# A one-core graph attention layer: the second head group's end cut into two and two target tiles, the guard moved from a product into the division, and the loop's order dealt anew

## What is computed

```python
h = relu(layernorm(x))
msg = h_neigh[None] + E[edge_types]      # edge_types = adj, so E[1] wherever an edge exists
q = h @ Wq.T + bq;  k = msg @ Wk.T + bk;  v = msg @ Wv.T + bv       # 8 heads x 16
scores = einsum(q, k) / 4, set to -1e9 where adj == 0
attn = softmax(scores) over the neighbours, 0 where adj == 0
out = x + einsum(attn, v).reshape(512, 128) @ Wo.T + bo
```

## Time and profile before

| | |
|---|---|
| three runs | 49.55, 49.84, 50.02 us |
| profiled execution | 49.53 us, span 47.7 us |
| busy | PE 42.2, DVE 39.1, ACT 33.6, POOL 30.0 us |
| first A-score of the stack (L622) | 14.82 us |
| first exponential | 17.59 us |
| last maximum ends | 33.39 us |
| last masked score ends | 40.16 us |
| last turn back ends | 44.70 us |
| last DMA issue | 45.59 us |

### The profile page before, as it was taken

How to read it: one execution, slowest core, us unless ns; L and a number is a source line. 1 busy time by engine, 2 the same in 40 slices (tenths; PEclk the granted TensorE clock), 3 DMA queues, 4 the chain that set the end, 5 groups by cost and what they waited for, 6 DMA issues and landing times.

```text
span 47.7 us, 834 instructions
## 1 busy us (share of the span) xinstructions
PE 42.2 (88%) x253; PEld 17.9 (37%) x256; DVE 39.1 (82%) x110; ACT 33.6 (70%) x60; POOL 30.0 (63%) x53
## 2 busy tenths in 40 slices
PE   0799996889997999999999999999999999999800
PEld 0323234365325244244544352252412233476500
DVE  2694696786898999999999999899788969999400
ACT  0293528689998759999999999599759999200410
POOL 5881005089996999484858579990899999800000
DMA  0499998980099999910000000000000000000032
GB/s 0 81 317 449 399 311 180 406 376 22 0 215 194 192 283 206 204 31 0 0 0 0 7 0 7 0 0 14 0 0 0 0 0 0 0 14 0 0 139 81
DMA packets 2071, 4.93 MB, mean 103 GB/s; under 512 B 258, under 2 KB 786, under 8 KB 1810
## 3 DMA queue, kind: packets, MB, share of 16 engines
q1 hardware_dynamic: 1490, 2.38, 21.2%
q10 hardware_dynamic: 576, 2.49, 13.9%
HBM read 3.02 MB, written 0.26 MB: 69 GB/s over the span
## 4 chain that ended last, share of the span: by engine, by line
PE 65%; DVE 17%; ACT 9%; issue 3%; DVEq 0%
PE ps L655 15%; PE ps L622 10%; PE ps L547 8%; PE ps L672 8%; PE ps L610 7%; DVE masked_scores L476 4%; PE ps L630 4%; PE ps L650 3%; ACT prob L395 3%; DVE turned_U L502 3%; DVE scaled L506 3%; DVE masked_n L491 3%; PE ps L556 2%; DVE ctxT L515 2%; PE ps L578 1%
## 5 line engine op out<-in xcount | busy, mean ns | idle before, releaser
L476 DVE CUSTOM_DVE_ANT_0 masked_scores<-ps,mask_b 128x512 bf16<-128x512 f32 x32 | 19.9, 687 | 0.5 <-PE ps L610 0.3
L260 POOL TENSOR_TENSOR prob<-prob,live 128x512 int32<-128x512 int32 x11 | 13.9, 1279 | 0.0
L395 ACT ACTIVATE prob<-ps 128x512 f32<-128x512 f32 x23 | 12.2, 599 | 1.0 <-PE ps L655 0.8
L655 PE MATMUL ps<-stack 98*128 98x512 bf16 x32 | 11.0, 381 | 0.3 <-issue 0.2
L622 PE MATMUL ps<-stack 96*128 96x512 bf16 x28 | 9.8, 379 | 0.4 <-DMA stack<-split 0.3
L491 DVE TENSOR_TENSOR masked_n<-ps,veto 128x512 f32<-128x512 f32 x9 | 5.7, 684 | 1.0 <-PE ps L655 1.0
L395 ACT ACTIVATE prob<-masked_n 128x512 f32<-128x512 f32 x9 | 5.2, 624 | 1.0 <-DVE masked_n L491 1.0
L236 POOL COPY split<-split 128x512 int32<-128x512 int32 (+1 forms) x4 | 1.9, 508 | 5.4 <-ACT split L333 3.9
L547 PE MATMUL ps<-ones 128*128 128x512 bf16 x9 | 4.0, 628 | 1.4 <-DVE ones L414 1.4
L655 PEld LDWEIGHTS ps<-stack 98*128 98x128 bf16 x32 | 3.1, 97 | 5.2 <-ACT stack L366 1.3
L366 ACT ACTIVATE stack<-ps 2x512 bf16<-2x512 f32 x8 | 4.7, 590 | 0.4
(11 more groups left out here) (73 smaller groups left out, 56.7 us busy)
## 6 DMA issues: line engine op xcount, KB each, us to landing
stack<-split SPq DMA_DIRECT2D x8, 192.0 KB, 4.0
adj_b_sb<-adj_b_dram ACTq DMA_DIRECT2D x1, 1024.0 KB, 7.1
adj_n_sb<-adj_n_dram ACTq DMA_DIRECT2D x1, 1024.0 KB, 10.0
pk<-pack_k_dram ACTq DMA_DIRECT2D x1, 322.0 KB, 3.7
xt<-x_dram SPq DMA_DIRECT2D x1, 256.0 KB, 3.5
pw<-pack_w_dram SPq DMA_DIRECT2D x1, 192.0 KB, 4.9
out_dram<-y SPq DMA_DIRECT2D x1, 192.0 KB, 1.9
brow<-bias_rows_dram SPq DMA_DIRECT2D x1, 128.0 KB, 8.3
```

The costliest lines, as they stand in the source:

```text
L260: nc.gpsimd.tensor_tensor(bits, bits, live[:, LIVE_TILES.index(t), :], ALU.mult).then_inc(cut_done, 1)
L395: nc.scalar.activation(prob[:, h, t, :], scores, ACT.Exp, scale=DH ** -0.5).then_inc(exp_done, 1)
L476: nc.vector.tensor_tensor_reduce(out=masked_scores[:, k % len(A_BANKS), :], in0=ps[:, A_BANKS[k % len(A_BANKS)], :], in1=mask_b[:, t, :], ...
L655: nc.tensor.matmul(bank, stack[0:rows_of(h), h, SIDE["k"], t * P:(t + 1) * P], stack[0:rows_of(h), h, SIDE["q"], :], start=(h, t) not in O ...
```

## The change

It has five parts. (1) The second group's pieces are two and two target tiles instead of three and one. (2) `add_tiny` and its three products, two memsets and semaphores are gone; instead the scaling becomes one instruction that takes the minimum of the reciprocal and 1e30 and multiplies; the accumulation's start flag moves to the first step. (3) One warm-up product fewer. (4) In the front, `take_k_away(0)` goes between the two halves of the queries' projection, `project_v` ahead of `take_q_away(0, (0,))`, and on DVE `make_mask_b(1)` ahead of the third Q part and `make_mask_b(2)` ahead of the first maximum. (5) The tables of the loop: POOL cuts ten tiles and not eleven, PE adds thirteen vetoes and not twelve, DVE still masks nine, all of them now behind the last maximum; the steps of the first product come later, its last one behind all B-scores, and the first step of the last group's piece 1 comes earlier; POOL adds the output bias ahead of `split_max(3)` instead of at its end.

```diff
@@ -21,7 +21,8 @@
 FLOOR = -(2.0**29)
-TINY = 1e-30
+MOST = 1e30
 EPS = 1e-5
@@ -31,12 +32,12 @@
-PIECES = ((0, 3), (3, BT - 3))
+PIECES = ((0, 2), (2, BT - 2))
 HALVES = 2
...
 TAIL_ACC, TAIL_OUT = (0, 3), (4, 5)
-WARM_UP = 9
+WARM_UP = 8
@@ -44,22 +45,22 @@
 LIVE_TILES = (1, 3)
-ON_POOL = [(0, 1), (1, 1), (1, 3), (0, 3), (3, 3), (2, 3), (3, 1), (2, 1), (5, 1), (4, 1), (4, 3)]
-ON_DVE = [ORDER[18]] + [ORDER[24]] + [ORDER[23]] + ORDER[25:29] + ORDER[30:32]
+ON_POOL = [(0, 1), (1, 1), (0, 3), (2, 3), (3, 1), (2, 1), (5, 1), (4, 3), (4, 1), (6, 1)]
+ON_DVE = ORDER[22:26] + ORDER[27:32]
 ON_PE = [tile for tile in ORDER if tile not in ON_POOL and tile not in ON_DVE]
-A_BEFORE = (9, 9, 10, 12, 13, 14, 16, 17, 17, 19, 20, 20, 21, 23, 23, 25, 26, 27, 27, 28, 29, 31)
-ODD_VETOES = (1, 3)
+A_BEFORE = (10, 10, 13, 13, 13, 15, 16, 17, 18, 18, 20, 20, 22, 22, 23, 25, 27, 27, 28, 29, 31)
+ODD_VETOES = (3, 1)
 TURNS = ((0,), (1,), (2,), (3,), (4,), (5,), (6,), (7,))
-TURN_AT = ((0, 7), (3, 11), (6, 15), (10, 19), (14, 23), (18, 27), (22, 32), (25, 32))
-PLACED_AT = {1: 2, 2: 5, 3: 9, 4: 13, 5: 17, 6: 20, 7: 22}
-V_FIRST, V_LAST = (2, 0, 3, 1), ((0, 1, 2, 3), (3, 0, 2, 1))
-FIRST_AT = ((20, 28), (22, 32), (25, 32), (29, 32))
+TURN_AT = ((0, 8), (2, 12), (5, 15), (10, 20), (14, 23), (19, 28), (22, 32), (25, 32))
+PLACED_AT = {1: 1, 2: 4, 3: 9, 4: 13, 5: 17, 6: 21, 7: 22}
+V_FIRST, V_LAST = (0, 3, 1, 2), ((0, 1, 2, 3), (0, 3, 2, 1))
+FIRST_AT = ((23, 32), (25, 32), (28, 32))
...
@@ -208,12 +206,9 @@
             nc.gpsimd.memset(eps[:, :], EPS).then_inc(eps_set, 1)
-            nc.gpsimd.memset(tiny_row[:, :], 0.0).then_inc(tiny_zero, 1)
             nc.gpsimd.memset(ident16[:, :], 0.0)
...
             nc.gpsimd.memset(minus16[:, :], 0.0).then_inc(idents_zero, 1)
-            pool.wait_ge(tiny_zero, 1)
-            nc.gpsimd.memset(tiny_row[:, DH:P:CT], TINY).then_inc(tiny_set, 1)
             pool.wait_ge(idents_zero, 1)
@@ -294,23 +289,22 @@
             cut(0, 1)
+            add_out_bias()
             split_max(3)
...
             pool.wait_ge(live_ready, 2)
-            cut(1, 3)
+            cut(0, 3)
+            cut(2, 3)
             split_max(5)
-            cut(0, 3)
-            cut(3, 3)
+            cut(3, 1)
             split_max(6)
-            cut(2, 3)
+            cut(2, 1)
             split_max(7)
-            cut(3, 1)
-            cut(2, 1)
             cut(5, 1)
+            cut(4, 3)
             cut(4, 1)
-            cut(4, 3)
-            add_out_bias()
+            cut(6, 1)
@@ -462,8 +456,9 @@
                 q32_ready[1], 1)
+            make_mask_b(1)
             take_q_part(2)
-            make_mask_b(1)
+            make_mask_b(2)
@@ -493,8 +488,6 @@
                 find_max(0, t)
-                if t == 0:
-                    make_mask_b(2)
             def normalise(step, bank, g, first, tiles):
@@ -503,10 +496,10 @@
                 dve.wait_ge(recip_ready, step + 1)
-                nc.vector.tensor_tensor(
-                    scaled[:, blocks, g * DH:(g + 1) * DH], turned_U[:, g, blocks, 0:DH],
+                nc.vector.scalar_tensor_tensor(
+                    scaled[:, blocks, g * DH:(g + 1) * DH],
                     recip[:, g, blocks].rearrange("p (k c) -> p k c", c=1).to_broadcast([P, tiles * P // CT, DH]),
-                    ALU.mult).then_inc(u_scaled, 1)
+                    MOST, turned_U[:, g, blocks, 0:DH], ALU.min, ALU.mult).then_inc(u_scaled, 1)
@@ -516,21 +509,22 @@
-            for k in range(4, 28):
+            for k in range(4, 12):
+                find_max(k // BT, k % BT)
+            make_odd_veto(3)
+            for k in range(12, 32):
                 find_max(k // BT, k % BT)
             dve.wait_ge(veto_even_ready, 1)
-            mask_scores(*ORDER[18])
-            for k in range(28, 32):
-                find_max(k // BT, k % BT)
+            dve.wait_ge(veto_odd_ready, 1)
+            mask_scores(*ORDER[22])
             make_odd_veto(1)
-            make_odd_veto(3)
             dve.wait_ge(veto_odd_ready, 2)
+            mask_scores(*ORDER[23])
             mask_scores(*ORDER[24])
-            mask_scores(*ORDER[23])
             mask_scores(*ORDER[25])
-            mask_scores(*ORDER[26])
             mask_scores(*ORDER[27])
             mask_scores(*ORDER[28])
+            mask_scores(*ORDER[29])
             mask_scores(*ORDER[30])
@@ -546,12 +540,6 @@
-            def add_tiny(bank, columns):
-                pe.wait_ge(tiny_set, 1)
-                nc.tensor.matmul(ps[:, bank, 0:columns], tiny_row[0:1, :], ones[0:1, 0:columns], start=True, stop=False,
-                                 skip_group_check=True)
-            add_tiny(ACC_BANK, B)
             pe.wait_ge(msg_ready, 1)
@@ -588,13 +576,17 @@
             pe.wait_ge(pw_loaded, 16)
-            for i in range(HALVES):
+            def project_q(i):
                 pe.wait_ge(hT_ready[i], 1)
...
                                  skip_group_check=True).then_inc(q_projected[i], 1)
+            project_q(0)
             take_k_away(0)
+            project_q(1)
+            project_v((0, 1))
             take_q_away(0, (0,))
-            project_v((0, 1))
             take_k_away(1)
@@ -670,7 +662,7 @@
                     last = nc.tensor.matmul(ps[j * CT:(j + 1) * CT, ACC_BANK, :], V[:, t, j, :], prob[:, j, t, :],
-                                            start=False, stop=t == V_FIRST[-1], tile_position=(0, j * CT),
+                                            start=t == V_FIRST[0], stop=t == V_FIRST[-1], tile_position=(0, j * CT),
                                             skip_group_check=True)
@@ -680,8 +672,8 @@
                     last = nc.tensor.matmul(ps[j * CT:(j + 1) * CT, TAIL_ACC[i], 0:tiles * P], V[:, t, HG + j, :],
-                                            prob[:, HG + j, t, first * P:(first + tiles) * P], start=False,
-                                            stop=t == V_LAST[i][-1], tile_position=(0, j * CT), skip_group_check=True)
+                                            prob[:, HG + j, t, first * P:(first + tiles) * P],
+                                            start=t == V_LAST[i][0], stop=t == V_LAST[i][-1], tile_position=(0, j * CT), skip_group_check=True)
                 if t == V_LAST[i][-1]:
@@ -704,11 +696,11 @@
-            for k in range(BT, 5):
+            for k in range(BT, 6):
                 score_by_target(k // BT, k % BT)
...
             pe.wait_ge(ones_loaded, 16)
-            sent = 5
+            sent = 6
@@ -727,17 +719,17 @@
-            score_places(0, 26)
+            score_places(0, 24)
             pe.wait_ge(max_found, H * BT)
-            for i in range(len(PIECES)):
-                add_tiny(TAIL_ACC[i], PIECES[i][1] * P)
-            score_places(27, 31)
+            score_places(25, 28)
+            last_product_with_v(1, 0)
+            score_places(29, 31)
             last_product_with_v(0, 0)
+            first_product_with_v(2)
             last_product_with_v(0, 1)
...
             last_product_with_v(1, 3)
-            last_product_with_v(1, 0)
             last_product_with_v(1, 2)
```

More of the change, by code:

```diff
@@ L134, in gnn_kernel @@
         turned_U = sb("turned_U", [P, G, B // CT, CT])
-        tiny_row = sb("tiny_row", [1, P], bf16)
         recip = sb("recip", [P, G, B // CT])
@@ L181, in gnn_kernel @@
             sem("u_turned"), sem("recip_ready"), sem("u_scaled"), sem("ctx_ready"))
-        tiny_zero, tiny_set = sem("tiny_zero"), sem("tiny_set")
         out_projected, resid_ready, y_ready = sem("out_projected"), sem("resid_ready"), sem("y_ready")
```

## The result

The changed kernel has a median of 50.94 us in four runs, beside 49.93 for the kernel before: a ratio of 1.021, 95% interval 1.015 to 1.027. Run again later beside its variants it had 50.83 against 49.80, 1.023 (1.018 to 1.028). I had forecast 49.9 with a range to 50.5; it is slower, by a cause that was not among my rivals. The profiled execution took 51.16 us (span 49.4), against 49.53 (47.7).

What follows compares the result with a forecast made beforehand. Bound: small dependent steps until 15 us, PE to 38.9, then DVE to 44.70. Front 0, loop 0, end on DVE -0.3, projection +0.24, copy +0.11, store +0.07: +0.1, forecast 49.9 us, no change, range 49.1 to 50.5.

Steps and rivals of the forecast that it cites:

- (f): DVE behind the last maximum: 5.96 us of work from 33.1, plus waits for PE, ending at 40.1 against 40.16.
- The front, taken as 0: Before head 0's scores: the earlier keys' projection and the reordering cancel, so scores start at 10.92 as before.
- g: Gain from starting the keys' projection earlier: 0.22 us, or 0.55 at the high clock; scores move by 0.31 - g.
- First exponential 0.5 us later: ACT in the loop: first exponential at 18.1, not 17.59, waiting on maximum 6; even again by exponential 22.
- The starving of the loop: Rival, chance 0.17: late exponentials on ACT hold up PE's scores and open DVE's chain of maxima; 50.4 us.
- the late score: Late in the loop: A-score 23 reaches DVE 0.2 us late, leaving the last maximum's end at 33.1.
- The end on DVE: normalise(0) starts at 40.1, its scaling takes 0.43 instead of 0.77, last turn back at 44.4: -0.3 us.
- The projection: At the end, the last piece of two tiles is projected in 0.74 us against 0.50 for one: +0.24.
- the copy: At the end, copying 256 columns takes 0.39 us against 0.28 for 128: +0.11.
- Nothing is won up to here: Up to the last masked score: PE's savings return as waits; DVE and the first group's last step end at 40.1.
- The clock, 0.06: Rival, chance 0.06: PE's idle piece in the front puts off the clock's rise past 8 us; about +1, 50.9.
- What would show me wrong: Sign: the masks on DVE end more than 0.4 us from 40.1.

Runs made afterwards that it cites:

- Without the collision: Changed kernel with POOL waiting for the second odd veto before its cuts behind the last maximum's split: 49.97 us, ratio 1.006 to the kernel before.
- the front repaired: Changed kernel with POOL waiting for the second odd veto and the front's order as before: 49.74 us against 49.80, ratio 1.002.
- the single repair: Changed kernel with only the front's order and mask tiles as before, warm-up and guard products still out: 50.56 us, ratio 1.019 to the kernel before.
- a similar stall: Kernel before with its two odd vetoes moved behind the first late masked score, where POOL cuts: 51.48 to 53.12 us against 49.66.

## Why the prediction was wrong

The step that failed is (f), DVE's work behind the maxima: "0.38 + 9 x 0.62 = 5.96 us of work". The veto's 0.38 is its price where POOL cuts nothing, as at 33.31 in the earlier trace rows. In the changed kernel it took 1.54, and the last masked score ended 7.97 us behind the last maximum, not 7.0. I moved it, with that price, to behind a masked score, where the last maximum has just set POOL free, and did not ask what POOL does there. In the prediction's own part on the end I used the Trainium skill (SBUF — State Buffer, "SBUF: two separate sides") for the scaling beside POOL's bias. The same section of the Trainium skill names DVE's two-port modes as excluded by a POOL instruction too. The trace agrees as far as it goes: the veto took 1.54 and 1.55 us with a cut started just before, 0.42 without; that it runs in such a mode no row says. I applied the rule where the change removed a collision and not where it made one.

- *The front, taken as 0:* +0.30 measured, inside the bound for g = 0 (0.31) and outside what I took. The price of the reordering was right and the gain was not: from the end of `msgT` to ACT's first part of K it took 1.73 us against 1.78, so g was 0.05 in that run. `msgT` is also later in most runs than in the profile I read, so less PE time was there to win.
- *First exponential 0.5 us later:* right, 7.20 us behind head 0's scores against 6.67. *The starving of the loop, a rival at 0.17:* did not happen; DVE lost about 0.4 us in its chain of maxima at two places. The last maximum came 22.27 us behind head 0's scores; forecast 22.2, with 0.2 for the late score.
- *The end on DVE:* scaling 0.42 (0.43), 4.30 us in all (4.3). The 0.34 taken off the scaling is right, though in the kernel before it came back as a wait. *The projection* 0.73 (0.74), *the copy* 0.38 (0.39), the store of 128 KB 1.7 us (1.75 to 1.8).
- *"Nothing is won up to here":* right once the collision is gone, 7.07 against 7.0.
- *The clock, 0.06:* not in the changed kernel's profile beyond the keys' projection, but in three profiles of its variants the projection took 2.07 us. Three of the ten profiles with eight warm-ups speak for a larger chance than 0.06.
- *What would show me wrong:* masks more than 0.4 us from 40.1. They ended at 41.72, of which 0.56 came from ahead of the loop.

Without the collision the forecast of 49.9 would have held (49.97, and 49.74 with the front repaired). In these two profiles it took 34.86 and 34.85 us from head 0's scores to the last DMA issue, against 34.67 before: 0.18 more, where the sum had some 0.05, so the sum there was good to 0.15. What stays open is how the loss of the front divides between the order and the clock in the medians: the single repair lies within its interval.

## What to carry to other kernels

When an instruction is moved on one engine, look up what the other engines do at its new place, and take its price from a row with the same neighbours; for VectorE, look at GpSimd. A row much longer than its like and without idle time before it may be a stalled instruction and not work: hold the neighbour back, as POOL was here, and see whether it shrinks. A cut into pieces and an order of products must be judged together: the same cut of two and two cost 0.27 us in one order (0.42 by its profile) and saved about 0.25 in the other (by the profiles alone).

## What the runs showed that was not expected

- One stalled VectorE instruction of 1.1 us cost the whole kernel 0.8 to 1.0 us although TensorE was the fuller engine, since TensorE's scores wait for banks that VectorE empties.
- It held in the other direction too: POOL's cut that stood behind the first one took 1.46 us, from 35.49, where the others took 1.28; the veto ended at 35.81.
- In the kernel before, a similar stall left TensorE idle for 1.82 us, and in the profiled execution the granted clock then fell to 0.71 and 0.50 over the next 4 us. With 1.2 us of stall and 0.6 of a longer wait, the execution whose clock stayed up was 1.8 us over the kernel before, and the three others 3.2.
- The keys' projection took 1.21 to 1.93 us, and 2.16 or 2.17 in three profiles, from the end of `msgT` to ACT's first read of it. `msgT` itself started 4.41 to 4.93 us after the span's start, as `pk` landed. Head 0's scores started at 10.82 to 12.37 us in the profiles; how the spread of the unprofiled executions divides is not shown.
